# Second biases gathered per token and added in the first expert; first weight chunk split in halves; first picks in three banks

## The reference

```python
gate_logits = h2 @ Wg
w, sel = jax.lax.top_k(gate_logits, K)            # K = 1
w = jax.nn.softmax(w)                             # 1 for K = 1
combine = zeros.at[arange(n)[:, None], sel].add(w)
hid = jax.nn.relu(jnp.einsum('nd,edf->enf', h2, W1) + b1[:, None, :])
y = jnp.einsum('enf,efd->end', hid, W2) + b2[:, None, :]
moe = jnp.einsum('ne,end->nd', combine, y)
return x + moe
```

## Time and profile before

| | us |
|---|---|
| Median of 3 runs | 882.34 |
| Lowest and highest run | 880.31, 886.64 |
| Time of the profiled execution | 882.35 |
| Span of the profiled execution (first to last instruction) | 880.8 |
| First product of expert 0 begins | 428.68 |
| Last product of expert 7 ends | 866.40 |
| From there to the end | 14.4 |

### The profile page before, as it was taken

One profiled execution on the slowest core, in us unless ns is written; L12 is line 12 of the kernel. 1 busy time (PEld: TensorE's weight loads), 2 busy tenths in 40 slices (PEclk: granted clock), 3 DMA queues, 4 the chain that ended last, 5 costly groups with the idle time before them and its releaser, 6 DMA issues.

```text
span 880.8 us, 14635 instructions
## 1 busy us (share of the span) xinstructions
PE 846.6 (96%) x5326; PEld 815.4 (93%) x5326; DVE 713.1 (81%) x1102; ACT 552.9 (63%) x785; POOL 78.3 (9%) x85
## 2 busy tenths in 40 slices
PE   7999999989899998999989999999999999999997
PEld 7989999989789888898989999999999999999996
DVE  6999586873578787755788897998989899898996
ACT  4612341352577777614577877888878888787880
POOL 2000000230400000031600000000000000000041
PEclk9999999999999999999999999999999999999998
DMA  7030017162930033430799999999999999999984
GB/s 219 22 108 1 19 25 156 53 161 67 319 116 2 1 108 92 159 89 1 251 361 355 355 338 377 346 364 373 351 377 359 364 373 351 376 347 374 373 279 139
DMA packets 116232, 196.00 MB, mean 223 GB/s; under 512 B 34052, under 2 KB 83420, under 8 KB 116182
## 3 DMA queue, kind: packets, MB, share of 16 engines
q1 hardware_dynamic: 107858, 168.88, 56.4%
q0 software_dynamic: 6368, 24.19, 8.0%
q10 hardware_dynamic: 1956, 2.26, 1.0%
HBM read 177.40 MB, written 17.90 MB: 222 GB/s over the span
## 4 chain that ended last, share of the span: by engine, by line
PE 61%; DVE 19%; DMA 11%; issue 4%; ACT 4%; SPq 0%; DVEq 0%; ACTq 0%
PE ps L1502 12%; PE ps L1905 11%; DMA raw<-in_L_ffn_W 11%; PE ps L1924 10%; DVE wlo L1002 10%; PE ps L1686 7%; PE ps L1531 4%; PE ps L1757 3%; PE ps L1735 2%; PE ps L1582 2%; PE ps L1608 2%; PE ps L1720 2%; PE ps L1890 2%; ACT whi L668 2%; DVE ohs L1054 1%
## 5 line engine op out<-in xcount | busy, mean ns | idle before, releaser
L1002 DVE TENSOR_TENSOR wlo<-raw,whi 128x2304 fp32r<-128x2304 f32 (+1 forms) x150 | 352.7, 2359 | 22.8 <-ACT whi L668 22.4
L668 ACT ACTIVATE whi<-raw 128x2304 fp32r<-128x2304 f32 (+1 forms) x152 | 300.7, 1980 | 80.9 <-DMA raw<-in_L_ffn_W 33.7
L1924 PE MATMUL ps<-whi,hTT 128*128 128x384 f32 x768 | 201.5, 339 | 0.7 <-ACT oh7T L668 0.7
L1924 PEld LDWEIGHTS ps<-whi,hTT 128*128 128x128 f32 x768 | 139.1, 188 | 1.0 <-ACT oh7T L668 1.0
L1905 PE MATMUL ps<-whi,hgh 128*128 128x384 f32 x384 | 133.0, 346 | 1.0 <-DVE hgl L1002 1.0
L1924 PE MATMUL ps<-wlo,hTT 128*128 128x384 f32 x384 | 129.0, 336 | 0.0
L1905 PE MATMUL ps<-whi,hgl 128*128 128x384 f32 x384 | 129.0, 336 | 0.0
L1905 PE MATMUL ps<-wlo,hgh 128*128 128x384 f32 x384 | 128.4, 334 | 0.0
L1905 PEld LDWEIGHTS ps<-whi,hgh 128*128 128x128 f32 x384 | 72.2, 188 | 1.2 <-DVE hgl L1002 1.2
L1924 PEld LDWEIGHTS ps<-wlo,hTT 128*128 128x128 f32 x384 | 72.3, 188 | 0.0
L1905 PEld LDWEIGHTS ps<-wlo,hgh 128*128 128x128 f32 x384 | 72.3, 188 | 0.0
(11 more groups left out here) (294 smaller groups left out, 1589.2 us busy)
## 6 DMA issues: line engine op xcount, KB each, us to landing
raw<-in_L_ffn_W SPq DMA_DIRECT2D x128, 1152.0 KB, 6.9
hs_d<-bc POOLq DMA_DIRECT2D x13, 384.0 KB, 6.4
raw<-in_L_gnn_W SPq DMA_DIRECT2D x4, 1152.0 KB, 5.8
hs<-hs_d POOLq DMA_DIRECT2D x8, 384.0 KB, 5.6
ys_d<-ysb POOLq DMA_DIRECT2D x7, 384.0 KB, 5.9
raw<-in_L_ffn_Wv SPq DMA_DIRECT2D x6, 384.0 KB, 5.2
raw<-in_L_ffn_Wq SPq DMA_DIRECT2D x12, 192.0 KB, 3.6
raw<-in_L_ffn_Wk SPq DMA_DIRECT2D x12, 192.0 KB, 3.5
```

The source lines that it names most:

```text
L668: act.activation(out_, in_, func).then_inc(s, 1)
L1002: dve.tensor_tensor(out_, in_, hi_, ALU.subtract).then_inc(s, 1)
L1924: ins = mm(ps[0:CAP, 4 + half, 0:HB], l, rr, start=k == 0 and j == 0 and jj == 0, stop=k == FCH - 1 and j == JW - 1 and jj == 2)
```

## The change

1. **Second bias.** `b2` is no longer loaded and split, and the 20 products `bias_y` are gone, as are the turning and the copy of the marks of all experts (`oh8T`). Instead, GpSimd issues, after the first load of `hs`, five indirect gathers that put `b2[eidx]`, 125 rows of 3 KB each, in `x2` (free by then). VectorE adds each, weighted, to `base` in steps k = 9 to 13 of expert 0, and waits there until all five have landed.
2. **First chunk by halves.** ScalarE rounds chunk 0 in two halves. VectorE makes the rest of the first half before it waits for the gates, and that of the second half where the whole was. CHOICE_BUSY goes from 12 to 9.
3. **Picks in three banks.** Blocks m = 0, 1 go to bank 6, 2, 3 to bank 7, 4, 5 to bank 5, and `s_pick` is raised after m = 1 and m = 3, so that ScalarE begins on the first two blocks earlier.
4. **End.** Y_BACK_AT goes from 10 to 8, and the fifth block's `others_y` is made with the four others, ahead of the split of expert 7's output.

```diff
-Y_BACK_AT = 10
+Y_BACK_AT = 8
+B2_AT = 9
-TURN_BUSY, GATE_BUSY, RANK_BUSY, CHOICE_BUSY = 3, 3, 8, 12
+TURN_BUSY, GATE_BUSY, RANK_BUSY, CHOICE_BUSY = 3, 3, 8, 9
...
+        def picked(m):
+
+            return ps[0:128, (6, 7, 5)[m // 2], m % 2 * 128:m % 2 * 128 + CAP]
...
-            g.dma_start(bc[1][0:E, :], b2[:, :]).then_inc(s_b2in, 16)
...
             g.wait_ge(s_scat, 16 * C)
             next_in(0)
+            g.wait_ge(s_base, C)
+            for c in range(C):
+                g.indirect_dma_start(out=x2[:, c, :], out_offset=None, in_=b2[:, :],
+                                     in_offset=bass.IndirectOffsetOnAxis(ap=eidx[:, c:c + 1], axis=0)
+                                     ).then_inc(s_b2in, 16)
             with g.Fori(1, E) as t:
                 next_in(t)
                 y_out(t)
-            g.wait_ge(s_base, C)
+            g.wait_ge(s_b2, C)
             g.wait_ge(s_route, 1)
...
             a.wait_ge(s_x2, C)
-            split_hi(0, 0)
+            a.wait_ge(s_raw[0], FULL[0] + 16)
+            act.activation(whi[0][:, 0:CH // 2], raw[0][:, 0:CH // 2], ACT.Copy).then_inc(s_mhalf, 1)
+            hi(whi[0][:, CH // 2:CH], raw[0][:, CH // 2:CH], s_mhi)
...
-            a.wait_ge(s_pick, 1)
             for m in range(EARLY):
-                act.activation(hgf[:, m, :], blocks(6, 128, DC, CAP)[:, m, :], ACT.Identity,
+                a.wait_ge(s_pick, m // 2 + 1)
+                act.activation(hgf[:, m, :], picked(m), ACT.Identity,
...
-                        hi(oh8T[0:E, :, :], blocks(4, E, C, P), s_ohl)
                         hi(oh7T[:, :, :], blocks(6, 128, C, P), s_ohl)
...
-            a.wait_ge(s_b2in, 16)
-            a.wait_ge(s_used, SCH * (E - 1) + FCH + 6)
-            hi(b2h, bc[1][0:E, :], s_b2h)
...
+            d.wait_ge(s_mhalf, 1)
+            dve.tensor_tensor(wlo[0][:, 0:CH // 2], raw[0][:, 0:CH // 2], whi[0][:, 0:CH // 2], ALU.subtract)
             d.wait_ge(s_gate, 1)
...
-            split_lo(0, 0)
+            d.wait_ge(s_mhi, 1)
+            lo(wlo[0][:, CH // 2:CH], raw[0][:, CH // 2:CH], whi[0][:, CH // 2:CH], s_mlo)
             d.wait_ge(s_rank, 1)
...
+                    if first and B2_AT <= k < B2_AT + C:
+                        c = k - B2_AT
+                        d.wait_ge(s_b2in, 16 * C)
+                        d.wait_ge(s_base, C)
+                        dve.scalar_tensor_tensor(base[:, c, :], x2[:, c, :], wtok[:, c:c + 1], base[:, c, :],
+                                                 ALU.mult, ALU.add).then_inc(s_b2, 1)
...
-            d.wait_ge(s_b2h, 1)
-            lo(b2l, bc[1][0:E, :], b2h, s_b2l)
-            d.wait_ge(s_base, C)
+            d.wait_ge(s_b2, C)
...
-            for c in range(C - 1):
+            for c in range(C):
                 others_y(c)
...
-            others_y(C - 1)
...
-                if m == EARLY - 1:
+                if m % 2 and m < EARLY:
                     ins.then_inc(s_pick, 1)
...
-                for c in range(C):
-                    ins = nc.tensor.transpose(blocks(4, E, C, P)[:, c, :], rt[:, 3, c * E:(c + 1) * E], ident[0:P, 0:P])
                 ins.then_inc(s_ohT, 1)
...
-                    pe.wait_ge(s_ohl, 2)
+                    pe.wait_ge(s_ohl, 1)
...
-            def bias_y(c, half):
-                for i, t in enumerate((b2h, b2l)):
-                    mm(ps[0:P, LAST_BANK[c] + half, 0:HB], oh8T[0:E, c, :], t[:, half * HB:(half + 1) * HB],
-                       start=i == 0, stop=False)
...
-            pe.wait_ge(s_b2l, 1)
             pe.wait_ge(s_hga, DC * (E + 1) - EARLY)
             for half in range(2):
-                for c in range(3):
-                    bias_y(c, half)
                 pe.wait_ge(s_yl, half + 1)
...
-                    bias_y(c, half)
                     spread_y(c, half).then_inc(s_sel, 1)
```

More of the change, by code:

```diff
@@ L211, in build @@
                     [("n2", [P, C, D], F32), ("h2T", [128, DC, NP], F32)],
-                    [("oh7T", [128, C, P], F32R), ("oh8T", [128, C, P], F32R),
-                     ("r3pad", [128, RB - 2 * C * P - 2 * DF // 128 * CAP], F32),
+                    [("oh7T", [128, C, P], F32R),
+                     ("r3pad", [128, RB - C * P - 2 * DF // 128 * CAP], F32),
                      ("hTT", [128, FCH, 2, JW, CAP], F32R)])
@@ L241, in build @@
         rt, tp, iotac, oh0 = R2["rt"], R1["tp"], R2["iotac"], R1["oh0"]
-        oh7T, oh8T, hTT = R3["oh7T"], R3["oh8T"], R3["hTT"]
+        oh7T, hTT = R3["oh7T"], R3["hTT"]
         def hTT_part(i, n):
             return hTT[:, FCH - 1 - n, i, :, :]
-        b2h, b2l = whi[1][0:E, 0:D], wlo[1][0:E, 0:D]
         ps = ctx.enter_context(nc.psum_tensor("ps", [128, 8, 512], F32))
@@ L385, in build @@
         s_scat = sem("tokens_sent")
-        s_b2in, s_b2h, s_b2l = sem("b2_in"), sem("b2_hi"), sem("b2_lo")
+        s_b2in, s_b2 = sem("b2_rows_in"), sem("b2_rows_added")
         s_pick, s_ea, s_eh, s_el = (sem(n) for n in (
@@ L391, in build @@
         s_used, s_mhi, s_mlo = (sem(n) for n in ("chunks_used", "expert_hi", "expert_lo"))
+        s_mhalf = sem("first_expert_half_hi")
         s_hidev, s_hidT, s_bia, s_hTh2, s_hTl2 = (sem(n) for n in (
@@ L929, in _ @@
             hi(hg[0][:, 0:EARLY, :], hgf[:, 0:EARLY, :], s_eh)
-            tile_part(1, range(EARLY, DC))
+            a.wait_ge(s_hgT, 1)
+            for m in range(EARLY, DC):
+                act.activation(hgf[:, m, :], picked(m), ACT.Identity,
+                               scale=lnT[:, 2 * DC + m:2 * DC + m + 1],
+                               bias=lnT[:, 3 * DC + m:3 * DC + m + 1]).then_inc(s_hga, 1)
             a.wait_ge(s_hga, DC - EARLY)
@@ L1865, in _ @@
                 for c in range(C):
-                    ins = mm(blocks(6, 128, DC, CAP)[:, m, :], n2[:, c, m * 128:(m + 1) * 128], oh0[:, c, :],
+                    ins = mm(picked(m), n2[:, c, m * 128:(m + 1) * 128], oh0[:, c, :],
                              start=c == 0, stop=c == C - 1)
-                if m == EARLY - 1:
+                if m % 2 and m < EARLY:
                     ins.then_inc(s_pick, 1)
@@ L1875, in marks_turned @@
                 for c in range(C):
-                    nc.tensor.transpose(blocks(6, 128, C, P)[:, c, :], oh0[:, c, :], ident[0:P, 0:P])
-                for c in range(C):
-                    ins = nc.tensor.transpose(blocks(4, E, C, P)[:, c, :], rt[:, 3, c * E:(c + 1) * E], ident[0:P, 0:P])
+                    ins = nc.tensor.transpose(blocks(6, 128, C, P)[:, c, :], oh0[:, c, :], ident[0:P, 0:P])
                 ins.then_inc(s_ohT, 1)
@@ L1945, in spread_y @@
                     ins = mm(ps[0:P, LAST_BANK[c] + half, 0:HB], oh7T[:, c, :], t[0:CAP, half * HB:(half + 1) * HB],
-                             start=False, stop=i == 1)
+                             start=i == 0, stop=i == 1)
                 return ins
-            pe.wait_ge(s_b2l, 1)
             pe.wait_ge(s_hga, DC * (E + 1) - EARLY)
             for half in range(2):
-                for c in range(3):
-                    bias_y(c, half)
                 pe.wait_ge(s_yl, half + 1)
```

## The result

| | us |
|---|---|
| Kernel before, median of 4 runs beside it | 882.0 |
| Changed kernel, median of 4 runs | 897.95 (893.8 to 900.71) |
| Ratio, with its 95% interval | 1.0173, 1.0139 to 1.0207 |
| Span of the profiled execution, before and after | 880.8, 899.2 |

The account below looks back on a forecast made before the run. TensorE and DMA were taken as both full, with VectorE's chain of rests and loads setting the pace early in the experts. From 882.35 us, -1.25 + 4.2 - 2.9 gave 882.4, rounded down to 882.0, range 880 to 884.5.

Parts of the forecast that it names:

- Start: First chunk's rest by halves, ahead of the gates: everything behind its second half comes 1.24 us sooner, counted as -1.25 us.
- the forecast 427.4: Start of the first expert: its first product was to begin near 427.4 us.
- Change 3 and the marks: Picks in three banks: 0, covered by VectorE's two rests; turnings of the marks dropped: 0, at most -0.7 us.
- The gathers, traffic: Weight loads beside the b2 gathers: 5.1 us of traffic, 1.6 into a gap, at least 3.5 us pushed back.
- The gathers, wait: VectorE before the additions in expert 0: fifth gather landed at 469.5 (bounds 461.7 to 475.7), a wait of 1.2 us.
- late gathers: Rival, expert 0: fifth gather lands at 475.7, delaying the rests and the loads behind; 887 us, chance 0.12.
- The additions: VectorE in expert 0: five additions of 1.01 us, each ahead of one rest; chunk 13's rest +3.8 us, wait included.
- Change 4 at nothing: Expert 7: y gathers two chunks sooner cost 0, with 4.3 us in hand and under half of the DMA used.
- that rival: Rival, expert 7: the earlier y gathers hold up the last chunks by more than 4.3 us; 884 us, chance 0.07.
- The end: After the last product, without bias products: -2.9 us, between 1.6 and 3.8 gained, with the output's transfers becoming late next.
- The length of an issue: GpSimd's gather issues: long beside VectorE's rests (median 2.74 us), where the skill's rule would make all five short.
- early gathers: Rival, expert 0: short issues, landing by 465, VectorE doesn't wait and only traffic counts; 878 to 880 us, chance 0.27.

Follow-up runs that it names:

- e12: The kernel before with scatters and y gathers of 128 rows instead of 125, nothing else changed: 878.80 us, ratio 0.9964.
- e14: e12 with the first chunk by halves, 9 fill products and the picks in three banks: 880.66 us, ratio 0.9984.
- e3: e1 with the b2 gathers, but without VectorE's five additions and its wait for the gathers: 892.02 us, ratio 1.0109.
- e2: e1 without the b2 gathers and without the additions of b2: 878.12 us, ratio 0.9961.
- e5: e1 with each b2 and y gather 128 rows long instead of 125: 884.58 us, ratio 1.0026.
- e4: e1 with the five additions, but without the b2 gathers and the wait for them: 880.41 us, ratio 0.9994.
- e1: The changed kernel with the y gathers issued at 10 used chunks of expert 7 again: 893.61 us, ratio 1.0140.
- e10: e5 with b2 gathers of 127 rows instead of 128, y gathers left at 128: 907.69 us, ratio 1.0283.

## Why the prediction was wrong, point by point

**Start (change 2, -1.25 us): right up to the first product.** The first half fitted ahead of the gates. VectorE read the gate values at 412.52 (412.62 in the earlier trace rows), and the first product of expert 0 began at 427.38:

```profile
412.52 0.19 DVE L1336 TENSOR_TENSOR rt<-ps,rt 125x40 f32<-125x40 f32 x1
```

```profile
427.38 0.44 PE L1919 MATMUL ps<-whi,hgh 128*128 128x384 f32 x1 [1.32 <-DVE hgl L1012]
```

From one to the other it is 14.86 us, where it was 16.06. In e12, which doesn't have the halves, it is 16.06 again, and in all the other traces 14.84 to 15.04. So 1.2 us are gained up to the first product. That it fell on the forecast 427.4 is luck beside that, since both points move by over 3 us from one execution to the next. The picks ended at 426.05, 1.1 us sooner than I wrote. That the 1.2 us reach the end of the kernel is not shown (e14).

**Change 3 and the marks: no place found where they cost or gave anything,** as written; no run takes them out alone.

**The gathers, traffic: the step that failed.** The sum put "1.92 MB at the 374 GB/s of a full stretch", 5.1 us, of which 1.6 fell into a gap. It priced a gather by its bytes. Measured, the gathers alone (e3 against e2) cost 13.9 us, and nearly the same bytes in 128 rows (e5 against e4, which also differ in the rows of the y gathers) 4.2 us (2.8 by the ratios, since the two ran on different chips), near the 3.5 of the sum. So the price by volume was about right for a transfer of 128 rows, and wrong by a factor of 3 to 4 for these. The rows had the hint: the scatters of 125 rows took 9.0 to 12.8 us to land, the y gathers, most of them alone on the queues, 8.0 us for 0.38 MB, which is 48 GB/s for each; I took that for the latency of the kind. In e5 the y gathers of 128 rows landed in 5.7 us.

**The gathers, wait: named, but undersized.** VectorE waited 5.25 us, not 1.2, and the last landing at 477.6 was past the upper bound of 475.7 that I had made from the scatters. The rival "late gathers" had the right place, but the wrong mechanism: it let the landing delay VectorE, and left the weight loads as they were. e3 shows that without VectorE's wait the time hardly changes.

**The additions: 2.3 us (e4 against e2, intervals that overlap),** where the walk had about 3.8 with the wait.

**Change 4 at nothing: wrong, by the same step.** "Gathers of 2.7 us per 384 KB take under half of the DMA" was again a price by bytes. The loads, with 4.3 us in hand, took 7.5 and 11.0 us longer to land (13.1 and 16.6 us from issue, 5.6 before), and TensorE waited; that rival had 884 us and 0.07.

**The end: -1.8 us in place of -2.9.** The changed kernel's last product begins here:

```profile
886.29 0.34 PE L1938 MATMUL ps<-whi,hTT 128*128 128x384 f32 x1
887.73 0.41 PE L1954 MATMUL ps<-whi,oh7T 128*125 128x384 f32 x1 [1.10 <-DVE wlo L1012]
```

```profile
882.39 4.73 DVE L1469 SCALAR_TENSOR_TENSOR base<-x,wtok,base 125x768 f32<-125x768 f32 x5
887.03 1.01 DVE L1012 TENSOR_TENSOR wlo<-ps,whi 128x384 fp32r<-128x384 f32 x2
888.42 5.34 DVE L1482 SCALAR_TENSOR_TENSOR base<-ps,wtok,base 125x384 f32<-125x384 f32 x10 [0.38 <-PE ps L1954]
```

The ten additions took 5.34 us from start to end, 0.53 each as the better of my two values. But they began at 888.42, 1.8 us after the last product, and not 1.1: the late last chunk had pushed the five `others_y` behind it. And the output transfers became late next, as suspected: from the last addition to the end 5.4 us passed, where it had been 4.0.

**The length of an issue.** The first two b2 gathers were issued in 1.2 us, the others in 3.1 to 3.5, each of these begun while VectorE made a rest. That is what the earlier trace rows said, and not what the inference of the Trainium skill (SBUF — State Buffer, Who interferes with whom) on `tensor_tensor` would give: by it all five would have been short. The rows show that the two go together, not why. It didn't decide anything here.

The rival "early gathers" had a slip in its sum: the 2 to 2.3 us that it took for the traffic held the -1.25 of the start already, which it then took off once more. Its own terms give -1.3 to -2.6, so 880 to 881 and not 878 to 880. That didn't touch the forecast.

Of the chances: 0.05 stood on slower by over 1%, which is what happened. All bounds of the unknown cost came from transfers of the same odd shape beside a less full queue, or from bandwidth; none from a row that showed what such a transfer does to its neighbours. One was at hand: the loads issued beside the scatters, from 428 to 447 us, had landed in 9.1 to 10.9 us, those issued from 456 to 467 us in 5.4 to 6.4. It was a hint only, for the load at 472.66 took 8.37 with no indirect transfer beside it.

## What to carry to other kernels

Price a transfer beside a full weight stream by what its shape does to the others' landing, not by its bytes: look at how long the neighbours' loads take to land beside a transfer of the same kind and row count. Give indirect transfers 128 rows where a tile has 125, even if three rows are thrown away; it was worth 9 us in e1 here (e5) and made the kernel before 0.4% faster. And put a new transfer where the queues are idle before asking how to hide it.

## What the runs showed of the hardware that I had not expected

- An indirect gather of 125 rows of 3 KB beside full queues lowered the whole core's traffic from some 357 to 275 GB/s, at a DMA share above 1 (e2, e3); at 128 rows it stayed at 381 (e5). A DMA share of 1 doesn't say that the engines carry all that they could.
- 127 rows are worse than 125 and 120: 23.1, 9.0 and 4.8 us over 128 rows in this kernel, VectorE's wait for the gathers (19.52 us at 127) counted in.
- In e10 TensorE stood still for 24.8 us; in the windows shown, 476 and 484 us, the granted clock was 0.50, and the DMA share 0.53 and 0.35 with transfers still waited for.
